# Output projection and attention residual computed for pairs of tiles: eight products with 256 moving columns from a two-tile buffer of O, in place of eight with 128 for every tile

## What is computed

```python
x = attn_layer(shift_tokens(x), Wqkv[i], q_scale[i], k_scale[i], Wo[i]) + x
x = ffn_layer(shift_tokens(x), ln_g[i], ln_b[i], W1[i], b1[i], W2[i], b2[i]) + x
```

## Time and profile before

| | |
|---|---|
| median of 3 runs | 3281.72 us (3278.72 to 3283.54) |
| profiled execution: span from first to last instruction | 3281.1 us |
| TensorE busy | 3130.3 us (95%) |
| VectorE busy | 2721.8 us (83%) |
| ScalarE busy | 2486.3 us (76%) |
| GpSimd busy | 2434.9 us (74%) |
| mean granted TensorE clock | 0.992 of full speed |

### The profile page before, as it was taken

One profiled execution on the slowest core, in us unless ns is written; L12 is line 12 of the kernel. 1 busy time (PEld: TensorE's weight loads), 2 busy tenths in 40 slices (PEclk: granted clock), 3 DMA queues, 4 the chain that ended last, 5 costly groups with the idle time before them and its releaser, 6 DMA issues.

```text
span 3281.1 us, 120591 instructions
## 1 busy us (share of the span) xinstructions
PE 3130.3 (95%) x51702; PEld 2520.7 (77%) x51702; DVE 2721.8 (83%) x3169; ACT 2486.3 (76%) x3160; POOL 2434.9 (74%) x1229
## 2 busy tenths in 40 slices
PE   7999999999999999998888999999999999999999
PEld 5888888888888887875333788888788888888787
DVE  7887888888888888877999888888888888888886
ACT  5777777787777777777676777778777778778776
POOL 6787787776776776762999778778768768778664
PEclk8999999999999999999999999999999999999999
DMA  3333233233233332231000323323323323323222
GB/s 121 89 80 87 71 93 86 68 91 86 72 88 85 75 84 66 71 75 42 20 0 1 98 67 80 91 72 85 92 72 81 94 71 81 97 66 90 69 67 66
DMA packets 142300, 245.23 MB, mean 75 GB/s; under 512 B 32397, under 2 KB 34638, under 8 KB 141774
## 3 DMA queue, kind: packets, MB, share of 16 engines
q1 hardware_dynamic: 141774, 237.51, 28.5%
HBM read 35.01 MB, written 1.05 MB: 11 GB/s over the span
## 4 chain that ended last, share of the span: by engine, by line
PE 84%; issue 5%; DVE 5%; POOL 3%; ACT 3%; DMA 0%; SPq 0%; ACTq 0%; DVEq 0%; POOLq 0%
PE PS L283 16%; PE PS L407 12%; PE PS L427 8%; PE PS L352 8%; PE PS L215 8%; PE PS L217 7%; PE PS L216 7%; PE PS L564 4%; PE PS L506 2%; PE PS L508 2%; PE PS L507 2%; PE PS L362 2%; PE PS L450 2%; POOL ARENA L1893 2%; DVE ARENA L1706 2%
## 5 line engine op out<-in xcount | busy, mean ns | idle before, releaser
L283 PE MATMUL PS<-C,ARENA 128*128 128x128 f32 x4608 | 619.7, 278 | 38.4 <-ACT ARENA L1025 11.4
L1777 POOL TENSOR_TENSOR ARENA<-ARENA 128x1024 f32<-128x1024 f32 x192 | 470.5, 2451 | 235.3 <-DVE ARENA L1359 234.5
L1785 POOL TENSOR_TENSOR ARENA<-ARENA,RN 128x1024 f32<-128x1024 f32 x192 | 365.3, 1903 | 367.7 <-ACT RN L960 367.7
L283 PEld LDWEIGHTS PS<-C,ARENA 128*128 128x128 f32 x4608 | 512.4, 141 | 119.1 <-issue 77.8
L1025 ACT ACTIVATE ARENA<-PS 64x1024 f32<-64x1024 f32 x384 | 390.5, 1017 | 182.2 <-PE PS L283 180.0
L215 PE MATMUL PS<-WL,XH 128*128 128x512 f32 x1152 | 500.0, 434 | 8.4 <-POOL XL L1744 4.0
L1771 POOL TENSOR_TENSOR ARENA<-ARENA 128x1024 f32<-128x1024 f32 x192 | 456.2, 2376 | 7.0 <-DVE ARENA L1341 7.0
L217 PE MATMUL PS<-WH,XH 128*128 128x512 f32 x1152 | 454.7, 395 | 0.1
L216 PE MATMUL PS<-WH,XL 128*128 128x512 f32 x1152 | 452.2, 393 | 0.0
L407 PE MATMUL PS<-ARENA 128*64 128x64 f32 x12288 | 403.0, 224 | 27.4 <-DVE ARENA L1399 14.0
L407 PEld LDWEIGHTS PS<-ARENA 128*64 128x64 f32 x12288 | 376.7, 138 | 60.8 <-issue 60.8
(11 more groups left out here) (163 smaller groups left out, 6419.1 us busy)
## 6 DMA issues: line engine op xcount, KB each, us to landing
ARENA<-ARENA SPq DMA_DIRECT2D x1152, 128.0 KB, 2.4
ARENA<-ARENA SPq DMA_DIRECT2D x768, 64.0 KB, 2.1
ARENA<-in_wqkv SPq DMA_DIRECT2D x36, 512.0 KB, 5.4
ARENA<-in_wo SPq DMA_DIRECT2D x12, 512.0 KB, 3.8
ARENA<-in_w SPq DMA_DIRECT2D x12, 341.0 KB, 3.1
ARENA<-in_w SPq DMA_DIRECT2D x12, 192.0 KB, 4.6
X<-in_xT SPq DMA_DIRECT2D x4, 256.0 KB, 4.6
out<-X SPq DMA_DIRECT2D x1, 768.0 KB, 3.3
```

The costliest lines, as they stand in the source:

```text
L283: last = nc.tensor.transpose(PS[:, slot, 128 * j:128 * j + 128], src[:, 128 * j:128 * j + 128], ident)
L1777: nc.gpsimd.tensor_tensor(KN[n % 2], KN[n % 2], T2, ALU.add).then_inc(k_add, 1)
```

## The change

The copy of O goes into a new buffer OP that holds two tiles, interleaved by 128-feature block j, so that block j of both tiles is 256 contiguous columns. `out_project` does nothing for even n and, for odd n, multiplies both tiles with 256 moving columns. `residual` does the same on VectorE with 256 columns, and adds 2 to `res_done`. Waits on `wo_done` count pairs, waits on `res_done` are rounded to pairs (`after_pair`). In the closing part of each stack, the products of tiles 92 and 94 are left out and those of 93 and 95 do the pair. A scratch area for DMAs is declared smaller, which makes room for OP.

```diff
+        OP = sb("OP", [128, 2048])
...
+            def after_pair(eng, sem, n):
+                if n >= 1:
+                    eng.wait_ge(sem, n0 + 2 * ((min(n, N - 1) + 1) // 2))
...
-                after_tile(pe, res_done, s - 23)
+                after_pair(pe, res_done, s - 23)
...
             def out_products(n, bank):
                 w = WO[n // NT % 2]
                 for j in range(8):
-                    last = nc.tensor.matmul(PSB[:, bank, 0:128], w[:, 128 * j:128 * j + 128], OTS[:, 128 * j:128 * j + 128],
+                    last = nc.tensor.matmul(PSB[:, bank, 0:256], w[:, 128 * j:128 * j + 128], OP[:, 256 * j:256 * j + 256],
                                             start=j == 0, stop=j == 7)
                 last.then_inc(wo_done, 1)
 
             def out_project(n):
-                if not 0 <= n < N:
+                if not 0 <= n < N or n % 2 == 0:
                     return
                 pe.wait_ge(oT_ev, n0 + n + 1)
-                if n % NT == 0:
+                if n % NT == 1:
...
-                tile(oT_ev, 92)
-                tile(res_done, 91)
                 units(f_ln, u)
-                out_products(92, 2)
...
-                out_products(94, 2)
                 units(f_sq, u + 1)
...
-                if n >= 1:
-                    act.wait_ge(wo_done, n0 + n)
-                act.activation(OTS, PS[:, 3, :], ACT.Copy).then_inc(oT_ev, 1)
+                if n >= 2:
+                    act.wait_ge(wo_done, n0 // 2 + n // 2)
+                act.activation(OP.rearrange("p (j t x) -> p j t x", j=8, t=2)[:, :, n % 2, :],
+                               PS[:, 3, :].rearrange("p (j x) -> p j x", j=8), ACT.Copy).then_inc(oT_ev, 1)
...
             def residual(n):
-                if not 0 <= n < N:
-                    return
-                q0 = 128 * (n % NT)
-                dve.wait_ge(wo_done, n0 + n + 1)
-                nc.vector.tensor_tensor(B[0:64, q0:q0 + 128], PSB[0:64, 2, 0:128], A[0:64, q0:q0 + 128], ALU.add)
-                nc.vector.tensor_tensor(B[64:128, q0 + 1:q0 + 129], PSB[64:128, 2, 0:128], A[64:128, q0 + 1:q0 + 129],
-                                        ALU.add).then_inc(res_done, 1)
+                if not 0 <= n < N or n % 2 == 0:
+                    return
+                q0 = 128 * (n % NT - 1)
+                dve.wait_ge(wo_done, (n0 + n + 1) // 2)
+                nc.vector.tensor_tensor(B[0:64, q0:q0 + 256], PSB[0:64, 2, 0:256], A[0:64, q0:q0 + 256], ALU.add)
+                nc.vector.tensor_tensor(B[64:128, q0 + 1:q0 + 257], PSB[64:128, 2, 0:256], A[64:128, q0 + 1:q0 + 257],
+                                        ALU.add).then_inc(res_done, 2)
...
-                    sp.wait_ge(wo_done, n0 + NT * l)
+                    sp.wait_ge(wo_done, (n0 + NT * l) // 2)
...
-    nc = _bacc.Bacc("TRN2", target_bir_lowering=False, num_devices=1)
+    nc = _bacc.Bacc("TRN2", target_bir_lowering=False, num_devices=1, dynamic_dma_scratch_size=1024)
```

More of the change, by code:

```diff
@@ L444, in out_project @@
                     after_tile(pe, kT_ev, s - 21)
-                    after_tile(pe, res_done, s - 24)
+                    after_pair(pe, res_done, s - 24)
                 out_products(n, 2)
@@ L615, in finish_tiles @@
                 tile(oT_ev, 93)
-                tile(res_done, 92)
+                tile(res_done, 91)
                 out_products(93, 2)
@@ L649, in finish_tiles @@
                 tile(oT_ev, 95)
-                tile(res_done, 94)
                 out_products(95, 2)
```

## The result

The changed kernel takes 3418.4 us (median of 4 runs, 3413.3 to 3420.8) against 3282.6 us for the kernel before on the same chip: ratio 1.041, 95% interval 1.040 to 1.042. It is 136 us slower. The forecast was 3395 (+113) with a range of 3350 to 3440.

What follows compares the result with a forecast made beforehand. TensorE, busy 95% of the span, was taken as the bound. From 3281.7 us: odd steps +137.8, even steps -26.2, first tiles -1.5, closing parts +5.2, clock -2, about +113, gave 3395 us; range 3350 to 3440.

Steps and rivals of the forecast that it cites:

- Part 1: Output product on TensorE: a pair's block takes 3.47 us against 3.57 before, saving 0.1 us a pair, 9 us in all.
- Rival B: Output product: weight loads are the bound, so a pair's block takes 1.79 us and the kernel 3252 us; chance 0.02.
- Part 2: Odd steps: the pair's whole product adds 1.68 us to TensorE in 82 steps, +137.8 us.
- ten absorbed: First odd step after a layer ends, five a stack: the wait ahead of `values` absorbs the added 1.68 us.
- -2 us for the clock: Layer steps: the longest wait, 3.67 us, shrinks to 2.0 us and the clock fall behind it may vanish, -2 us.
- Part 4: Smaller edits: residual, O's copy, weight-load waits and scratch area nothing; closing parts +5.2 us, clock -2 us.
- Part 3: Even steps: waits for P's copy and GpSimd's chain leave 0.57 us gained in n=2 (-26.2 us), nothing in n=0; first tiles -1.5.
- rival A: n=0 steps: TensorE's idle time of about 2.1 us lowers the clock each time, +44 to +66, 3440 to 3460 us; chance 0.09.
- 2.1 lies between, nearer to the harmless one: n=0 steps: idle 2.1 us lies between 1.7 us without a clock fall and 2.53 us with one, so likely no fall.
- the eight harmless ones: Waits of 1.7 us ahead of `values` in layer steps, eight times, said to bring no clock fall.
- C: Even steps: `q_transpose` doesn't follow P's copy, so the full 1.79 us comes back; 3273 us; chance 0.02.
- D: n=2 steps: other engines run ahead in longer odd steps and open the gates early, giving 56 us more, 3339 us; chance 0.07.

Runs made afterwards that it cites:

- experiment 6: Changed kernel with P's copy and the maximum's subtraction moved ahead, pair's products 128 columns wide against 256, on one chip: 3322.8 us narrow, 3311.1 us wide.
- experiment 3: Only the first of the two activations copying the transposed P, in both kernels: changed kernel 3335.9 us, kernel before 3266.3 us.
- experiment 1: Changed kernel plus four spare products where the output product of the n=0 steps was: 3385.1 us, ratio 1.032.
- experiment 5: Both kernels with P's copy before logarithm and exponential, subtract_max before normalisation; kernel before also with n=0 product behind Q's transpose: changed 3310.7 us, before 3261.1 us.

## Why the forecast was right, point by point

- **The product's price (Part 1).** A block of 3.47 us was forecast from a 217 ns spacing; 3.45 was measured, and 0.12 us saved a pair where 0.10 was forecast (experiment 6). Rival B (weight loads are the bound) and the estimate from the Trainium skill's page TensorE: Matmul & The Clock Gate, section Back-to-back issue gap, which would have put a pair's block near 2.1 us, are refuted for these f32 products.
- **Odd steps (Part 2).** For the steps in the table the forecast is 34 x 1.68 = 57.1 us for n=1 (ten absorbed) and 42 x 1.68 = 70.6 for n=3; measured 56.9 and 67.8. The ten layer steps did absorb it: eight waits are gone from the list and those steps are about 0.3 us longer; the two waits of 3.7 us shrank, and those steps are even 1.2 us shorter, since the low stretch behind each is gone. That is the -2 us for the clock in Part 4, and it came as forecast.
- **Even steps (Part 3).** n=0: nothing gained where the clock stays up, as forecast. n=2: 0.73 us in the median step instead of 0.57, which makes -32 instead of -25 in 44 steps; the measured -39 has 7 us more, from the steps with other waits named above. Tile 92 of each stack, which the forecast's list leaves out, behaves like n=0: the wait in its place grows from 0.58 to 2.60 us. The mechanism held, both gates are seen, with a third one as close (`subtract_max`, experiment 3); the latency behind GpSimd's chain was sized too large, 0.13 us where 0.06 was measured, and that chain itself ran a little shorter, 11.56 us from its first start (866.14) to its end against 11.63 before.
- **The clock (rival A), the term that was missed.** I had 0.09 on a fall in each n=0 step and nothing for the n=0 steps in the sum. The step that failed is "2.1 lies between, nearer to the harmless one". A low stretch followed in 27 of the 44 steps, and filling the gap gives 30 to 33 us back. The reasoning behind that step was wrong too: waits of 1.5 us, shorter than the eight harmless ones of 1.7, were followed by a low stretch in experiment 1.
- **C and D.** The cover was needed: halving the copy brought 83 us in the changed kernel and 17 in the other. D (the other engines run ahead and open the gates early) didn't happen; n=2 gained what its gates allowed.

That 3395 came within 23 us of the measurement is in part luck, because two misses have opposite signs. By the steps of the table the n=0 steps cost 35 us more than forecast, and the n=2 steps gave back 14 us more, half of that in steps with other waits, which the forecast didn't consider. With the clock's 30 to 33 us apart, the move itself costs 103 to 106 us, against 115 in the forecast without its 2 us for the clock. The two moves of experiment 5 show the place as the cause from the other side: they make the changed kernel about 107 us faster without touching its products, though some 30 us of that are the clock.

## What to carry to other kernels

Joining work of two pipeline steps into one saves what it saves, here 0.12 us a pair, and takes a cover away from every second step: before joining, look at which wait of the following item ended last in the step that is emptied, and subtract. A gate that is opened shows the next one, so name the whole row of them: here moving one item changed nothing and moving two brought about 107 us. And the emptied step pointed at something the kernel before could use too, a reordering worth 0.6% without any pairs.

## What the runs showed of the hardware that I had not expected

Waits of 2.1 us, on an engine busy before and after, were followed by the lower clock (1.2 GHz) in 27 of 44 cases, and the low stretch then fell on busy time: the `values` block behind it took 3.41 us instead of 2.02. The 24 extra stretches cost 30 to 33 us, 1.3 to 1.4 us each. The length of the wait doesn't decide it alone. The same wait of 2.1 us was followed by a low stretch in 16 of 22 steps of the first stack and in 11 of 22 of the second, with the same work; and of the four waits of 1.5 us at `values` late in the stacks, none was followed by one in the kernel before and two were in e1_filler. What decides it wasn't tested and stays open. Eight spare matmuls in the gap of n=0, which do nothing useful, left waits of about 0.3 us there, and no step n=0 but the two just named had a low stretch.
